# The square directly behind the spreading of values, gate 6 ahead of the fourth turn, small statistics steps at another place of GpSimd's program, and those of the first batch on VectorE

## The reference

```python
# conv, on the first layer norm's output (ln_c: mean and variance over axis 1, the channels)
xw = x.reshape(B, H // 8, 8, W // 8, 8, C).transpose(0, 1, 3, 2, 4, 5).reshape(-1, 64, C)
q, k, v = heads(xw @ Wq + bq), *heads(xw @ Wkv + bkv)          # 4 heads of 16
attn = softmax(q * scale @ k.T + rel_bias[index])
out = window_reverse(attn @ v @ Wproj + bproj).transpose(0, 3, 1, 2)
x = x + out
# ffn, on tokens of 64 channels
t = to_tokens(x); n = ln_t(t)                                  # ln_t: over the 64 channels of a token
p = softmax(n @ router_w + router_b); top_p, top_i = top_k(p, 2); top_p /= sum(top_p)
t = t + sum(top_p * (n @ expert_w[top_i] + expert_b[top_i]))   # 8 experts, 64 x 64 each
```

## Time and profile before

| | |
|---|---|
| time, median of 3 runs | 1330.58 us (1327.98 to 1331.97) |
| the profiled execution's own time | 1329.41 us |
| its span in the trace | 1327.6 us |
| TensorE busy | 1185.1 us, 89% of the span |
| VectorE busy | 1102.0 us, 83% |
| GpSimd busy | 1012.0 us, 76% |
| ScalarE busy | 890.9 us, 67% |
| mean share of full TensorE clock granted | 0.979 |

### The profile page before, as it was taken

How to read it: one execution, slowest core, us unless ns; L and a number is a source line. 1 busy time by engine, 2 the same in 40 slices (tenths; PEclk the granted TensorE clock), 3 DMA queues, 4 the chain that set the end, 5 groups by cost and what they waited for, 6 DMA issues and landing times.

```text
span 1327.6 us, 47504 instructions
## 1 busy us (share of the span) xinstructions
PE 1185.1 (89%) x19715; PEld 736.6 (55%) x19840; DVE 1102.0 (83%) x2362; ACT 890.9 (67%) x1679; POOL 1012.0 (76%) x873
## 2 busy tenths in 40 slices
PE   4579999998999999999899999999899999999975
PEld 3455655554565665555556556655555555556541
DVE  5458898898888889898888888989888888888874
ACT  5357777767666777767666777776667666766642
POOL 6467888878777888888777788887877777777652
PEclk8589999999999999999999999999999999999998
DMA  6012333322222233322222323331222222222221
GB/s 197 1 36 64 88 90 81 79 63 60 53 62 75 69 90 90 80 63 59 65 49 64 90 74 86 90 83 44 59 67 51 61 63 63 55 56 66 60 67 40
DMA packets 95621, 91.42 MB, mean 69 GB/s; under 512 B 26928, under 2 KB 62384, under 8 KB 95408
## 3 DMA queue, kind: packets, MB, share of 16 engines
q1 hardware_dynamic: 95408, 88.37, 26.3%
HBM read 35.90 MB, written 17.83 MB: 40 GB/s over the span
## 4 chain that ended last, share of the span: by engine, by line
PE 33%; ACT 25%; POOL 22%; DVE 13%; issue 7%; DMA 0%; POOLq 0%; SPq 0%; DVEq 0%; ACTq 0%
PE bank_y L527 9%; POOL t_g L1103 6%; PE bank_t L424 6%; ACT prob L671 6%; POOL prob L1081 5%; PE bank_s L409 5%; ACT v_bd L666 5%; POOL ln L1093 4%; DVE bank_e L877 3%; PE bank_g L516 3%; PE bank_s L383 3%; ACT y_out L713 3%; POOL t_n L1095 3%; ACT xc L683 3%; ACT g_copy L708 2%
## 5 line engine op out<-in xcount | busy, mean ns | idle before, releaser
L1103 POOL TENSOR_TENSOR t_g<-t_t,g_copy 128x512 f32<-128x512 f32 x128 | 165.1, 1290 | 184.7 <-ACT g_copy L708 184.4
L527 PE MATMUL bank_y<-t_g,w_exp 128*64 128x512 f32 x1024 | 263.9, 613 | 9.6 <-DVE t_g L953 4.5
L1081 POOL TENSOR_TENSOR prob<-prob,mx 128x512 f32<-128x512 f32 x256 | 261.5, 1042 | 13.8 <-DVE mx L845 13.2
L671 ACT ACTIVATE prob<-prob 128x512 f32<-128x512 f32 x256 | 162.9, 636 | 144.9 <-POOL prob L1081 143.3
L675 ACT ACTIVATE prob_t<-bank_t 128x512 f32<-128x512 f32 x256 | 153.7, 600 | 94.5 <-PE bank_t L424 94.4
L838 DVE TENSOR_TENSOR prob<-bank_s,rel 128x1024 f32<-128x1024 f32 x128 | 155.9, 1218 | 42.0 <-PE bank_s L409 42.0
L953 DVE TENSOR_TENSOR t_g<-t_t,bank_p 128x512 f32<-128x512 f32 x256 | 173.8, 679 | 8.4 <-PE bank_p L516 4.5
L424 PEld LDWEIGHTS bank_t<-idn,prob 128*128 128x128 f32 x1024 | 108.9, 142 | 123.7 <-issue 70.6
L424 PE MATMUL bank_t<-idn,prob 128*128 128x128 f32 x1024 | 168.6, 288 | 5.6 <-ACT prob_t L675 3.1
L845 DVE TENSOR_REDUCE mx<-prob 128x16 f32<-128x1024 f32 x128 | 154.8, 1209 | 0.1
L1093 POOL TENSOR_TENSOR ln<-ln,mhalf 128x8 f32<-128x8 f32 x64 | 105.5, 1649 | 64.3 <-DVE ln L879 64.3
(11 more groups left out here) (110 smaller groups left out, 2323.8 us busy)
## 6 DMA issues: line engine op xcount, KB each, us to landing
t_t<-t_rout SPq DMA_DIRECT2D x256, 128.0 KB, 2.4
x_in<-in_x SPq DMA_DIRECT2D x68, 256.0 KB, 3.3
r_b<-recip_rows SPq DMA_DIRECT2D x64, 256.0 KB
out_y<-y_out SPq DMA_DIRECT2D x128, 128.0 KB, 2.4
r_in<-sum_b SPq DMA_DIRECT2D x64, 16.0 KB
recip_rows<-r_out SPq DMA_DIRECT2D x64, 16.0 KB, 1.4
gate_sel<-in_sel SPq DMA_DIRECT2D x1, 512.0 KB, 3.6
rel<-in_relb SPq DMA_DIRECT2D x1, 256.0 KB, 2.8
```

What stands on the lines that cost most here:

```text
L527: mm(B_Y[C * a:C * a + C, :], w_exp[:, pair, :], t_g[:, (2 * pair + a) % TG, :], start=False, stop=(pair == MIXES // 2 - 1), skip_group_ch ...
L671: A(prob[:, i], prob[:, i], ACT.Exp).then_inc(p_ready.sem, 1)
L1081: G.tensor_tensor(sc, sc, mx[:, i, :].unsqueeze(2).broadcast_to([P, 2 * HEADS, NTOK]), ALU.subtract).then_inc(s_shifted.sem, 1)
L1103: G.tensor_tensor(t_g[:, u % TG, :], t_t[:, p, u % 2, :], g_copy[:, n % 2, :], ALU.mult).then_inc(tg_pool.sem, 1)
```

## The change

Five things are done, and the work computed stays the same.

1. TensorE: `gates(j-3, 6)` moves from behind the fourth turn and gate 5 to ahead of the fourth turn; ScalarE copies gate 6 ahead of the copy of the fourth turn. The gate matmuls get a semaphore for even and one for odd u.
2. ScalarE: the square of a strip moves from the head of the next slot to between `spread_values` and `exps(j+1, 1)`.
3. VectorE: `token_variance` is one instruction. xc2 has a 65th column that holds C times epsilon, the reduction goes over 65 columns into SBUF, and the division by C is made up for by the factor sqrt(C) at `copy_tokens`, as the scale of a copy that is made anyway. `add_input` moves ahead of gate 7.
4. GpSimd: in the PLANES slot `variances` moves from ahead of gate 6 to behind the two shifts; in the SCALES slot `deviations` and `scaled_means` move from ahead of those shifts to behind them. `normalise_input` waits for the scaled means by a semaphore of its own.
5. First image: VectorE does the ten small steps and both steps of xn for strip 0, and prepares the weights after that and no longer before.

```diff
-        xc2 = sb("xc2", [P, ROWS, C])
+        xc2 = sb("xc2", [P, ROWS, C + 1])
...
# TensorE, slot
                 if mixing:
                     experts(j - 3, 1)
+                if mixing:
+                    gates(j - 3, 6)
                 if attending:
                     turn_probs(j, 3, work)
                 if mixing:
                     gates(j - 3, 5)
-                    gates(j - 3, 6)
...
# ScalarE
-                A(t_rout[:, :], B_E[:, :], ACT.Copy).then_inc(tt_ready.sem, 1)
+                A(t_rout[:, :], B_E[:, :], ACT.Copy, scale=float(C) ** 0.5).then_inc(tt_ready.sem, 1)
...
-                if routing_on:
-                    square(j - 2)
...
+                if mixing:
+                    copy_gates(j - 3, 6)
                 if attending:
                     copy_probs(j, 3)
-                if mixing:
-                    copy_gates(j - 3, 6)
...
                     exps(j + 1, 0)
                     spread_values(j + 1, 1 - p)
+                if outputting:
+                    square(j - 1)
+                if projecting:
                     exps(j + 1, 1)
...
# VectorE
             def first_statistics(batch):
+
                 total_squares(batch)
                 total_planes(batch)
+                dve.wait_ge(totals.sem, totals.at(batch, 2))
+                V.tensor_scalar(st[:, 2, :], st[:, 0, :], 1.0 / C, None, ALU.mult).then_inc(variance.sem, 1)
...
                 turn_root(batch)
...
+                V.tensor_tensor(m_rstd[:, batch % 2, :], st[:, 2, :], r_std, ALU.mult).then_inc(mr_ready.sem, 1)
+                V.tensor_tensor(xn[:, :, :], xt[:, 0:4, :], rstd[:, 0:1, :].broadcast_to([P, 4, H]),
+                                ALU.mult).then_inc(xn_ready.sem, 1)
...
                 prepare_weights()
...
-                V.tensor_reduce(B_E[:, LN_AT + ROWS:LN_AT + 2 * ROWS], xc2[:, :, :], AX.X, ALU.add).then_inc(lvar.sem, 1)
-                dve.wait_ge(lvar.sem, lvar.at(g, 1))
-                V.tensor_scalar(ln[:, 2, :], B_E[:, LN_AT + ROWS:LN_AT + 2 * ROWS], 1.0 / C, LN_T_EPS, ALU.mult,
-                                ALU.add).then_inc(lvar.sem, 1)
+                V.tensor_reduce(ln[:, 2, :], xc2[:, :, :], AX.X, ALU.add).then_inc(lvar.sem, 1)
...
                     maxima(j + 1, 0)
+                if outputting:
+                    add_input(j - 1, 1 - p)
                 if mixing:
                     gate(j - 3, 1 - p, 7)
                 if outputting:
-                    add_input(j - 1, 1 - p)
                     token_mean(j - 1, 1 - p)
...
# GpSimd
                 if routing_on:
                     scale_tokens(j - 2)
+                if attending:
+                    shift(j, 2)
+                    shift(j, 3)
+                if work.step == PLANES:
+                    variances(work.batch)
                 if work.step == SCALES:
                     deviations(work.batch)
                     scaled_means(work.batch)
-                if attending:
-                    shift(j, 2)
-                    shift(j, 3)
...
                     normalise_input(j + 2)
-                if work.step == PLANES:
-                    variances(work.batch)
```

More of the change, by code:

```diff
@@ L212, in build @@
         xc2_ready = sem("xc2_ready")
-        lvar = sem("lvar", 2)
+        lvar = sem("lvar")
         lrstd = sem("lrstd")
@@ L225, in build @@
         gt_ready = sem("gt_ready")
-        gate_done = sem("gate_done", MIXES)
+        gate_done = [sem(f"gate_done{n}", MIXES // 2) for n in range(2)]
         g_copied = sem("g_copied", len(ON_POOL))
@@ L515, in gates @@
                     pe.wait_ge(tg_dve.sem, tg_dve.at(g, ON_DVE.index(u - 2) + 1))
-                mm(B_GATE[u % 2][:, :], gate_sel16[:, u, :], g_t[:, :], start=True, stop=True).then_inc(gate_done.sem, 1)
+                mm(B_GATE[u % 2][:, :], gate_sel16[:, u, :], g_t[:, :], start=True, stop=True
+                   ).then_inc(gate_done[u % 2].sem, 1)
             def experts(g, pair):
@@ L832, in first_statistics @@
                 total_planes(batch)
-                turn_root(batch)
+                dve.wait_ge(totals.sem, totals.at(batch, 2))
+                V.tensor_scalar(st[:, 2, :], st[:, 0, :], 1.0 / C, None, ALU.mult).then_inc(variance.sem, 1)
+                dve.wait_ge(variance.sem, variance.at(batch, 1))
+                V.tensor_tensor(st[:, 3, :], st[:, 2, :], st[:, 0, :], ALU.mult).then_inc(variance.sem, 1)
+                dve.wait_ge(variance.sem, variance.at(batch, 2))
+                V.tensor_tensor(st[:, 3, :], st[:, 1, :], st[:, 3, :], ALU.subtract).then_inc(variance.sem, 1)
@@ new lines, in first_statistics @@
+                dve.wait_ge(variance.sem, variance.at(batch, 3))
+                V.tensor_scalar(st[:, 4, :], st[:, 3, :], 0.0, 1.0 / C, ALU.max, ALU.mult).then_inc(variance.sem, 1)
+                dve.wait_ge(variance.sem, variance.at(batch, 4))
+                V.tensor_scalar(st[:, 4, :], st[:, 4, :], LN_C_EPS, None, ALU.add).then_inc(variance.sem, 1)
+                turn_root(batch)
+                r_std = rstd[:, batch % 2, :]
+                half, v = (st[:, n, :] for n in (3, 4))
+                dve.wait_ge(root_turned.sem, root_turned.at(batch, 1))
@@ new lines, in first_statistics @@
+                V.tensor_tensor(half, v, r_std, ALU.mult).then_inc(newton.sem, 1)
+                dve.wait_ge(newton.sem, newton.at(batch, 1))
+                V.tensor_tensor(half, half, r_std, ALU.mult).then_inc(newton.sem, 1)
+                dve.wait_ge(newton.sem, newton.at(batch, 2))
+                V.tensor_scalar(half, half, -0.5, 1.5, ALU.mult, ALU.add).then_inc(newton.sem, 1)
+                dve.wait_ge(newton.sem, newton.at(batch, 3))
+                V.tensor_tensor(r_std, r_std, half, ALU.mult).then_inc(rstd_ready.sem, 1)
@@ new lines, in first_statistics @@
+                dve.wait_ge(rstd_ready.sem, rstd_ready.at(batch, 1))
+                V.tensor_tensor(m_rstd[:, batch % 2, :], st[:, 2, :], r_std, ALU.mult).then_inc(mr_ready.sem, 1)
+                V.tensor_tensor(xn[:, :, :], xt[:, 0:4, :], rstd[:, 0:1, :].broadcast_to([P, 4, H]),
+                                ALU.mult).then_inc(xn_ready.sem, 1)
+                dve.wait_ge(mr_ready.sem, mr_ready.at(batch, 1))
+                dve.wait_ge(xn_ready.sem, xn_ready.at(0, 1))
+                V.tensor_tensor(xn[:, :, :], xn[:, :, :], m_rstd[:, 0:1, :].broadcast_to([P, 4, H]),
+                                ALU.subtract).then_inc(xn_ready.sem, 1)
@@ L1069, in normalise_input @@
                 par = (g % (2 * STRIPS)) // STRIPS
+                pool.wait_ge(mr_ready.sem, mr_ready.at(g // STRIPS, 1))
                 pool.wait_ge(qkv_done.sem, qkv_done.at(g))
@@ L1132, in slot @@
                     centre_tokens(j - 1, 1 - p)
-            def first_means(batch):
-                variances(batch)
-                deviations(batch)
-                scaled_means(batch)
-                normalise_input(0)
-            pipeline(pool, slot, add_planes, lambda batch: None, first_means)
-SET_DVE = 14
+            pipeline(pool, slot, add_planes, lambda batch: None, lambda batch: None)
+SET_DVE = 15
 SET_POOL = 1
```

9 lines of the change are left out of this document (5 added, 4 removed).

## The result

The changed kernel takes 1299.89 us (median of four runs, 1297.69 to 1300.69), the kernel before 1330.82 us in the same comparison: a ratio of 0.9768, with a 95% interval of 0.9748 to 0.9788. The forecast was 1284 us with a range of 1272 to 1304. The direction and the range hold, and the forecast's own value is 16 us too low. The profiled execution took 1299.60 us, its span is 1297.8.

The account below looks back on a forecast made before the run. No engine is full; a loop across engines, with VectorE's own chain ending last, sets the slot pace. Gains 13.5 + 13.5 + 12.0 + 4.5 + 3.0 = 46.5 us off 1329.4 give a median of 1284, range 1272 to 1304.

Parts of the forecast that it names:

- The square: Slots without extra work: an earlier square on ScalarE lets VectorE's variance reduction start earlier, by 0.39 us at most.
- Gate 5 0.2 us later: TensorE: gate 5 now stands behind gate 6 and the turn, charged 0.2 us on VectorE's chain; bounds nothing and 0.38.
- The addition's 0.12: VectorE: gate 7 between addition and mean fills the mean's wait for the addition's result, 0.12 us less.
- PLANES and SCALES slots: GpSimd's small steps move into a wait; gain 2.5 us per PLANES and 1.5 per SCALES slot, three each, 12.0 us.
- The start: First image: VectorE's small steps and xn take 4.5 us instead of 9.0 before TensorE's first projection, a gain of 4.5.
- first price: The start's cost basis: 128 x 128 results on VectorE took 0.29 us, against 0.56 beside a busy GpSimd.
- the tie: Plain slots: later gate 7 delays TensorE's scores 0.3 to 0.4 us, absorbed by 0.9 us of waits; scores just in time.
- The take slots: 27 slots with an earlier reduction and no second variance instruction: 0.50 us each, 13.5 us; lower bound 0.13.
- ties lost: Rival: the reciprocals and ScalarE's loop decide plain and take slots; gain 27.8 us, 1303 us, chance 0.18.
- The sign that had been set for gate 7: Sign of a wrong forecast: TensorE's last experts wait over 0.4 us for gate 7, then VectorE's second bias waits for scores.
- The slower rival: Gate 7 behind the addition delays TensorE's last experts, scores and VectorE's bias around the loop; 1341 us, chance 0.04.
- Filling and draining: Two filling and four draining slots have the chain through addition, mean and variance: 6 x 0.5 = 3.0 us.

Follow-up runs that it names:

- gate 7 first: The changed kernel with gate 7 put back ahead of the addition on VectorE: 1289.29 us, ratio 0.9690.
- both back: The changed kernel with gate 6 behind the fourth turn and gate 5 again and gate 7 ahead of the addition again: 1285.27 us, ratio 0.9663.

## Why the prediction came out as it did

**What held.** The square: VectorE's own chain was the limit, the reduction starts directly behind the bias, and the gain alone was 0.42, slightly above the 0.39 that the prediction called all that it can give. The second instruction: 0.20. Gate 5 0.2 us later: 0.17, from 0.64 to 0.81 us behind normalise, and the same by putting gate 6 back. The addition's 0.12: the mean starts 0.59 behind gate 7. PLANES and SCALES slots: 2.33 and 1.59 against 2.5 and 1.5. The start: 4.27 against 4.5. The rule that the prediction cited (the Trainium skill, "SBUF — State Buffer", "Who interferes with whom") agrees with the new rows: beside an idle GpSimd all 128 x 128 steps with two operands in SBUF took 0.29 us, and so did the weights' preparation, which had taken 0.56. The prediction's own first price did not show this: its instruction of 0.29 us at 1152.71 has one operand in a PSUM bank, and GpSimd was busy beside it (its power ran from 1151.56 for 1.65 us). The rule of the Trainium skill is for two inputs in SBUF and a GpSimd instruction that reads SBUF. So that row was another kind of instruction, and its price was the right one by luck.

**The step that failed** is the tie: "TensorE is then 0.3 to 0.4 us later with scores, values, sums and the keys' projection; this comes out of the two waits of 0.9 us together". The size was right, 0.31 us of wait for gate 7. What was wrong is that waits can be added up in this way. The two waits of the earlier trace rows are ahead of the turned gates and of the tokens, both fed from the variance and the routing; between the last experts and the second turn of the next slot stands another hand-over: scores, values, sums and the keys' projection on TensorE, then the copies k_m and prob_t on ScalarE, and then that turn. In the kernel before it looked like this, on the timelines of ScalarE and TensorE:

```profile
1152.38 0.59 ACT L675 ACTIVATE prob_t<-bank_t 128x512 f32<-128x512 f32 x1
1153.37 0.60 PE L424 MATMUL bank_t<-idn,prob 128*128 128x128 f32 x4
```

The copy ends at 1152.97. In the changed kernel the turn starts 0.14 us behind the end of this copy (1163.22 and 1163.36), so it could have started at 1153.11 here: this way had 0.26 us to spare, not 0.9. The later experts closed a loop of their own, in which the waits for the variance don't lie, and the loop runs through the very gate 5 that had been made 0.2 us late. Its length of 18.50 us hid all that the variance could gain beyond it: without the two moves a plain slot takes 18.25, which is 0.62 less than before, just the 0.42 and 0.20 of the two parts alone.

**The take slots** were the larger miss, 0.15 us for 0.50. (The 19.54 us that the prediction read is the last of nine take slots; most last 19.59.) Their lower bound of 0.13 holds by number, but its reason, a loop of TensorE and ScalarE at 19.4, was not what decided: with gate 7 first they run at 19.14, 0.45 less than before. The chance of "ties lost", 0.18, was too small, since its event (a tie on a loop that had not been written out) was more open than that; its two stated mechanisms, the reciprocals and ScalarE's loop, are both refuted as the cause. The result lies 3 us from that rival's 1303 and 16 from the forecast, and outside the forecast's own 1276 to 1292; it is in the stated range because its upper end, 1304, lies just above that rival, not because the sum was right. The sign that had been set for gate 7, a wait above 0.4 us followed by a wait of VectorE's second bias, did not come either: the wait is 0.31 us, and the second bias (1159.01) waits for nobody.

**The slower rival** named the right mechanism (gate 7 behind the addition), with a return of 0.6 us a slot in full. What came back was much less: against "gate 7 first" it is 0.08 us in plain and 0.30 in take slots, for the loop over gate 7 had slack before it became the longest.

**Filling and draining** gave 1.6 us of the 3.0: of the four intervals between the last starts of y_out three are 0.2 to 0.6 us longer and one is 2.35 shorter, and the last part of the span is only 1.1 us shorter.

## What to carry to other kernels

When a step is moved to a later place, write out the whole loop that passes through it, from its consumer back to itself one period later, and compare its length with the present pace; a wait elsewhere on the consumer's engine is slack only for a loop that passes through this wait. The gains of edits add while one loop carries them all (square and one instruction: 0.42 + 0.20 = 0.62), and two moves that gain 6.8 us alone can cost 14.3 in company, so each part is worth timing both alone and taken out. A wait that occurs in many slots, such as that for the reciprocals here, may still cost nothing: it is tried by taking it away.

## What the runs showed of the hardware that was not expected

SP takes unequal times to issue two DMAs of one form one behind the other. In the trace of "both back" the first store of a pair took 0.49 us at the middle and never more than 0.51; the second took 0.60 at the middle, but over 1 us in 8 of 64 slots, 1.80 in the slot shown above and 1.89 at most. Why it varies was not tried. The weights' preparation, moved behind xn to where GpSimd was idle, ran faster as well: its two SCALAR_TENSOR_TENSOR of 128 x 128 took 0.74 us together, where they had taken 2.61 beside a busy GpSimd. And the exponential behind a table load of 1.28 us starts 0.02 us after the load's end (621.20 + 1.28 to 622.50); the load showed no further cost than its own length in these rows.
